# Cross-attention and a mixture-of-experts layer on one core: the hand-over to the experts and the last sum, rearranged

## The reference, cut to what matters

```python
x = x + xattn(layernorm(x), ctx)              # x: (16, 256, 128), ctx: (16, 64, 128), 16 heads of 8
# softmax over the HEADS: attn = softmax(scores, axis=1)
h = layernorm(x)
raw = h @ centroids.T                          # 8 routed experts
scores, balanced = sigmoid(raw), sigmoid(raw + bias)
top_idx = top_k(balanced, 2)
top_w = softmax(gathered scores)               # two gates per token
x = x + h + shared(h) + sum_k top_w[k] * expert[top_idx[k]](h)
# an expert: gelu(h @ Wfc.T) @ Wproj.T, 128 -> 512 -> 128; two shared ones see every token
```

## Time and profile before

| what | value |
|---|---|
| runs | 399.82, 398.01, 400.16 us; median 399.82 |
| the profiled execution | 399.42 us, its span 397.5 us |
| busy PE / PEld | 313.9 us (79%) / 252.4 us |
| busy DVE / ACT / POOL | 288.0 / 259.7 / 260.2 us |
| mean granted TensorE clock | 0.943 |
| chain that ended last | PE 43%, DVE 20%, issue 17%, POOL 7%, ACT 6%, DMA 4% |

### The profile page before, as it was taken

One profiled execution on the slowest core, in us unless ns is written; L12 is line 12 of the kernel. 1 busy time (PEld: TensorE's weight loads), 2 busy tenths in 40 slices (PEclk: granted clock), 3 DMA queues, 4 the chain that ended last, 5 costly groups with the idle time before them and its releaser, 6 DMA issues.

```text
span 397.5 us, 11426 instructions
## 1 busy us (share of the span) xinstructions
PE 313.9 (79%) x3924; PEld 252.4 (63%) x3925; DVE 288.0 (72%) x596; ACT 259.7 (65%) x488; POOL 260.2 (65%) x268
## 2 busy tenths in 40 slices
PE   5865796577676639999999999799999999999100
PEld 1562464354444338888888776698998989999100
DVE  3779999988999967863749555567676667676167
ACT  2788799487686622856344789567666766767075
POOL 6254779789788591577777776057777777777500
PEclk9999899988989985999999999999999999999955
DMA  7956343400000000011112621313333232331097
GB/s 250 333 149 256 106 128 113 121 15 2 2 2 2 2 0 2 26 54 52 55 52 62 153 56 48 97 53 88 86 91 82 70 99 72 82 89 48 7 374 254
DMA packets 29176, 36.12 MB, mean 91 GB/s; under 512 B 4932, under 2 KB 24007, under 8 KB 28624
## 3 DMA queue, kind: packets, MB, share of 16 engines
q1 hardware_dynamic: 24592, 27.13, 22.2%
q0 software_dynamic: 4544, 8.44, 6.7%
HBM read 21.74 MB, written 14.72 MB: 92 GB/s over the span
## 4 chain that ended last, share of the span: by engine, by line
PE 43%; DVE 20%; issue 17%; POOL 7%; ACT 6%; DMA 4%; POOLq 1%; SPq 1%; DVEq 0%; ACTq 0%
PE banks L1454 9%; POOL results L507 7%; DVE Z L907 6%; DVE Mx L902 4%; PE banks L1438 3%; PE banks L1439 3%; PE banks L1440 3%; PE banks L1554 2%; PE banks L1556 2%; PE banks L1540 2%; PE banks L1558 2%; DVE X L1219 2%; ACT E L631 2%; PE banks L1344 2%; PE banks L1542 2%
## 5 line engine op out<-in xcount | busy, mean ns | idle before, releaser
L507 POOL DMA_INDIRECT results<-E,qRep x78 | 86.0, 1102 | 42.3 <-issue 27.4
L489 POOL DMA_INDIRECT gathered<-xs,slot x64 | 64.9, 1014 | 31.0 <-issue 18.6
L1190 DVE TENSOR_TENSOR E<-hid,E 128x512 f16<-128x512 f32 x78 | 54.0, 692 | 36.1 <-ACT E L774 36.1
L435 POOL TENSOR_TENSOR E<-E,rZ 128x1024 f32<-128x1024 f32 x32 | 67.4, 2129 | 18.4 <-DVE rZ L910 18.4
L772 ACT ACTIVATE hid<-banks 128x512 f32<-128x512 f32 x78 | 46.9, 602 | 38.0 <-DVE E L1190 22.6
L1554 PE MATMUL banks<-wprojL,E 128*128 x312 | 54.6, 219 | 2.9 <-DVE E L1190 1.8
L1558 PE MATMUL banks<-wprojH,E 128*128 x312 | 54.2, 219 | 0.0
L1556 PE MATMUL banks<-wprojH,E 128*128 x312 | 54.2, 219 | 0.0
L631 ACT ACTIVATE E<-banks 128x1024 f32<-128x1024 f32 x32 | 33.1, 1095 | 21.8 <-PE banks L1322 21.8
L774 ACT ACTIVATE E<-banks 128x512 f16<-128x512 f32 x78 | 47.2, 605 | 0.0
L1540 PE MATMUL banks<-qRep,wfcH 128*128 128x256 f16 x156 | 42.6, 273 | 0.8 <-ACT E L774 0.5
(11 more groups left out here) (218 smaller groups left out, 823.0 us busy)
## 6 DMA issues: line engine op xcount, KB each, us to landing
qRep<-gathered SPq DMA_DIRECT2D x39, 129.0 KB, 2.2
qRep<-q_rows SPq DMA_DIRECT2D x32, 128.0 KB, 2.5
qRep<-results SPq DMA_DIRECT2D x8, 512.0 KB, 7.3
X<-in_x SPq DMA_DIRECT2D x4, 512.0 KB, 6.6
q_rows<-qRep SPq DMA_DIRECT2D x8, 256.0 KB, 2.1
out<-X SPq DMA_DIRECT2D x8, 256.0 KB, 4.1
results<-E,qRep POOLq DMA_INDIRECT x78
gathered<-spare SPq DMA_DIRECT2D x9, 129.0 KB, 3.9
```

What stands on the lines that cost most here:

```text
L435: g.tensor_tensor(heads, heads, rZ[:, k % 2, :].unsqueeze(1).unsqueeze(3).broadcast_to([P, HH // 2, P, 2]), ALU.mult).then_inc(attn_ready, 1)
L489: g.indirect_dma_start(out=gathered, out_offset=bass.IndirectOffsetOnAxis(ap=slot[:, k, i:i + 1], axis=0), in_=xs[:, i, :], in_offset=None ...
L507: g.indirect_dma_start(out=results, out_offset=bass.IndirectOffsetOnAxis(ap=xg[:, k, h, 2 * D:ROW].bitcast(I32), axis=0), in_=yg[:, k, h, ...
L1190: v.tensor_tensor(gL[:, j, 2 * c:2 * c + 2], hid[:, 2 * j + c].rearrange("p (c q) -> p c q", c=2), gH[:, j, 2 * c:2 * c + 2], ALU.subtract ...
```

## The change

Four edits. (1) ScalarE's copy_o(14) goes ahead of the sigmoids' Exp and of all Gelus; copy_o(15) stays behind the four Gelus. (2) VectorE does scores_in(0) ahead of add_attention(13), and scores_in (for both portions) reads the scores out of PSUM twice, without the copy between. (3) ranks(0) goes from chunk 0 of the first shared expert to chunk 1. (4) For pairs 1 and 4, the last sum is made by TensorE: ScalarE makes 16 diagonal matrices ahead of time (identity times gate: two pairs, two gates, four tiles), TensorE adds X and both diagonal products in a PSUM bank (12 fp32 products a pair), and ScalarE copies the bank into X. VectorE's and ScalarE's own loops do the other six pairs; SP still stores in the order of the pairs.

```diff
+PE_PAIRS = (1, 4)
@@ sync
             for a in range(PAIRS):
-                sp.wait_ge(combined, a + 1)
+                summed = sum(p <= a for p in PE_PAIRS)
+                if a in PE_PAIRS:
+                    sp.wait_ge(copied, summed)
+                else:
+                    sp.wait_ge(combined, a + 1 - summed)
                 sp.dma_start(ov[:, a], Xo[:, a]).then_inc(stored, 16)
@@ scalar
-            sigmoid_exps(0)
-            gelu(0, 0, 0, False)
             act.wait_ge(y_ready, UNITS - 3)
             copy_o(UNITS - 2, 0)
-            for c in range(1, FC):
-                gelu(0, 0, c, False)
+            sigmoid_exps(0)
+            gelus(0, 0, False)
...
             act.wait_ge(gate_ready, 2)
+            for quarter in range(QUARTERS):
+                act.wait_ge(scattered[quarter], 16 * 2 * QT)
+            for n, a in enumerate(PE_PAIRS):
+                for k in range(2):
+                    for i in range(TP):
+                        last = s.activation(diag[:, n, k, i], ident[:], ACT.Identity, bias=zero[:],
+                                            scale=gate[:, k, a * TP + i:a * TP + i + 1])
+                last.then_inc(diag_ready, 1)
+
+            def copy_sum(n):
+                act.wait_ge(sum_ready, n + 1)
+                s.activation(X[:, PE_PAIRS[n]].rearrange("p b c d -> p (b c d)"), sum_ps[n], ACT.Copy).then_inc(copied, 1)
+
             for a in range(PAIRS):
+                if a in PE_PAIRS:
+                    continue
...
                 last.then_inc(gated, 1)
+                for n, b in enumerate(PE_PAIRS):
+                    if a == b + 2:
+                        copy_sum(n)
@@ vector
-            add_attention(UNITS - 3, 1, PAIRS - 2)
...
-                then(v.tensor_copy(rt[:, 0, t], raw))
-                v.tensor_copy(rt[:, 1, t], rt[:, 0, t]).then_inc(rneed, 1)
-                v.tensor_tensor(rt[:, 2, t], rt[:, 0, t], bias8[:].unsqueeze(1).broadcast_to(tok8), ALU.add
+                v.tensor_copy(rt[:, 1, t], raw).then_inc(rneed, 1)
+                v.tensor_tensor(rt[:, 2, t], raw, bias8[:].unsqueeze(1).broadcast_to(tok8), ALU.add
                                 ).then_inc(rneed, 1)
...
             scores_in(0)
+            add_attention(UNITS - 3, 1, PAIRS - 2)
             add_attention(UNITS - 2, 0, PAIRS - 1)
...
-            for a in range(PAIRS):
+            for n, a in enumerate(a for a in range(PAIRS) if a not in PE_PAIRS):
@@ tensor
-            shared_expert(0, 0, 0, 0, False, first=True, ranks_at=(0, 0))
+            shared_expert(0, 0, 0, 0, False, first=True, ranks_at=(0, 1))
...
+            for n, a in enumerate(PE_PAIRS):
+                pe.wait_ge(diag_ready, n + 1)
+                pe.wait_ge(acc_done, PAIRS)
+                pe.wait_ge(yk_loaded[a], 16)
+                for i in range(TP):
+                    o = sum_ps[n][:, P * i:P * i + P]
+                    t.matmul(o, ident[:], X[:, a, i // 2, i % 2, :], start=(i == 0), stop=False, skip_group_check=True)
+                    for k in range(2):
+                        last = t.matmul(o, diag[:, n, k, i], yk[:, a, k, i], start=False, stop=(i == TP - 1 and k == 1),
+                                        skip_group_check=True)
+                last.then_inc(sum_ready, 1)
```

More of the change, by code:

```diff
@@ L190, in xattn_moe_kernel @@
         sharedH, sharedL = (q_flat[:, at:at + 1024].rearrange("p (e n) -> p e n", e=SHARED) for at in (8192, 9216))
+        diag = xs_flat[:, 0:len(PE_PAIRS) * 2 * TP * P * 2].bitcast(F32).rearrange("p (a k i m) -> p a k i m", k=2, i=TP, m=P)
         iota8 = sb("iota8", [P, EXPERTS])
@@ L209, in xattn_moe_kernel @@
                            for i in (0, 1))
+        sum_ps = [banks[:, i, :] for i in range(len(PE_PAIRS))]
         up_ps = [banks[:, i, :] for i in (0, 1, 2, 3)]
@@ L263, in xattn_moe_kernel @@
         combined, combined_half = sem("combined"), sem("combined_half")
+        diag_ready, sum_ready, copied = sem("diag_ready"), sem("sum_ready"), sem("copied")
         stored = sem("stored")
@@ L1221, in _ @@
                 last.then_inc(combined_half, 1)
-                dve.wait_ge(combined_half, a + 1)
-                dve.wait_ge(gated, a + 1)
+                dve.wait_ge(combined_half, n + 1)
+                dve.wait_ge(gated, n + 1)
                 xv = X[:, a].rearrange("p b c d -> p (b c d)")
```

## The result

The changed kernel takes **393.23 us** (median of six runs, 391.42 to 395.13) against 399.48 (six runs, 397.96 to 400.39): a ratio of 0.9845, interval 0.9807 to 0.9883. Forecast were 392.8 in 391.0 to 396.0. The profiled executions took 399.42 and 391.42; the second is the fastest of its six, so the traces differ by more than the medians' 6.2 us. Where a kernel's runs fall into a fast and a slow group, a ratio here compares the fast ones alone and can differ from the quotient of the medians.

The account below looks back on a forecast made before the run. Two lines, TensorE's work and GpSimd's scatters, meet at the routed experts and were taken as the bound, so both must come earlier. 399.42 − 5.1 (earlier start there) − 1.5 (the end) = 392.8 us, range 391.0 to 396.0.

Parts of the forecast that it names:

- 5.1 + 1.5: Gains in us: routed experts start 5.1 earlier (3.5 to 6), and the end is 1.5 shorter.
- VectorE's two steps: scores_in, held by GpSimd at 1.31 and 2.15 us, would take 0.29 and 0.42 reading PSUM.
- ScalarE's order: At the hand-over, copy_o(14) first lets project_out(14) start at 143.5 instead of 149.21; copy_o(15) runs 147.3 to 147.7.
- TensorE's clock: A short clock fall at the hand-over: project_out(15) takes 2.08 us; TensorE's line gains 6.2 us (5 to 7).
- Choose beside GpSimd's small steps: At the hand-over, GpSimd's small steps delay VectorE's choice by 0 to 1.4 us, taken as 0.5.
- Slots: place(0)'s slots ready at 157.1 instead of 161.74, so the scatters' line gains 4.7 us (3.5 to 5.5).
- Which line sets the routed experts' start: The scatters' line sets it: loads land at 247.0, TensorE ready at 246.0, start 247.1 instead of 252.22.
- TensorE's first transpose waiting for it, not for VectorE: Sign at the routed experts' start: TensorE waits for SP's first load, issued at 244.5.
- hangs on these same two lines and moves along: The scatters' later waits, place(1) and the second token rows, were taken to shift with both lines, without separate price.
- The end: Two pairs summed on TensorE: last addition ends at 393.3 against 394.92; 1.5 us gained, bounds 1.6 loss to 2.3 gain.
- rival A's third case: At the end, the full DMA queue sets the time, so no gain there; 394.3 to 395.9 us; whole rival's chance 0.17.
- Rival D: TensorE's sum holds the end and the kernel gets slower, 401.4 us at 9 us a pair; chance 0.03.

Follow-up runs that it names:

- scores_alone: Kernel before plus only scores_in reading PSUM twice and going ahead of add_attention(13); ScalarE's order and ranks as before; profiled run 391.42 us.
- held_scores: Whole change, but scores_in copies out of PSUM once and works on that copy in SBUF, as before; profiled run 394.21 us.
- hand_only: Whole change without the sums on TensorE, the end as in the kernel before; ratio 0.9878 to the kernel before, 394.08 us.
- rows_later: Whole change with VectorE's second_rows(3) moved from behind half expert 11 to behind half expert 12; profiled run 391.24 us.
- plus_one3: rows_later, plus ScalarE instead of VectorE adding the 1 to the sigmoids' Exp, and copy_o(15) ahead of the fourth Gelu; profiled run 390.00 us.
- ranks_first: Whole change, but ranks(0) back in chunk 0 of the first shared expert, as before; profiled run 395.18 us.
- copy_alone: Kernel before plus only ScalarE's copy_o(14) ahead of the sigmoids and Gelus; profiled run 396.09 us.
- no_last_sum: Whole change with the last weighted sum left out, each store waiting for its load alone, output incomplete; profiled run 392.07 us.
- end_only: Kernel before plus only pairs 1 and 4 summed on TensorE, hand-over as before; ratio 0.9959, 396.79 us.

## Why the prediction was right, and where not

The time was forecast as 392.8 and came out at 393.2, by 5.1 + 1.5 where the traces have 5.6 + 1.3. Errors inside both terms partly cancelled, so that the sum came so close is in part luck (below).

- *VectorE's two steps.* Right: priced 0.29 and 0.42, measured 0.29 and 0.28, unheld, and the Exp came at M + 5.5, as by the forecast (copy_o(14) over at 143.5). scores_alone and held_scores show the hold as the cause.
- *ScalarE's order.* Right in each start, to 0.1 us. What the prediction did not work out is how the edits share the gain: it told the story of both holds and priced only their sum. Edit 2 alone gives 5.2, and edit 1 on top of it nearly nothing, since project_out(15) then starts at M + 9.69 with either order, behind GpSimd's last half.
- *TensorE's clock.* Wrong: a short fall was taken into the sum, and the clock stayed at 1.00 through the hand-over, in the change, hand_only, rows_later, plus_one3 and scores_alone. The first down products started 10.7 after M, not 11.8, and TensorE's line was 7.1 us ahead, not 6.2 and just beyond the upper bound of 7. It did fall where TensorE stood 1.9, 2.2 or 3.6 us: held_scores, ranks_first, copy_alone.
- *Choose beside GpSimd's small steps.* Over-priced: 0.5 taken, and from the end of its first step to the end of the choice it took 5.3 us, as before. GpSimd's steps grew instead: five of the fourteen took 0.25 to 0.29, one of them before. The first step's hold was foreseen (its end at M + 8.5, measured 8.56). The Trainium skill (SBUF — State Buffer, Who interferes with whom) fits what was measured of the long instructions, 1.40 for the tensor_scalar in SBUF, which the section counts among the operations that can take a two-port mode, and 2.24 for the sum with two SBUF inputs; of a hold by the small ones VectorE's durations show nothing.
- *Slots.* 4.7 to gain by the forecast, 5.4 measured; the difference is these two terms.
- *Which line sets the routed experts' start.* Wrong in its form: "TensorE's first transpose waiting for it, not for VectorE". TensorE waited for VectorE. The scatters did set the start, but through second_rows(3), a wait in VectorE's queue in front of the low halves that TensorE needs, which the prediction passed over as "hangs on these same two lines and moves along". It does move, with the scatters and not with TensorE, and passed TensorE's surplus back to it. rows_later takes it away, and then the load is what TensorE waits for. Here two errors cancelled: SP's first load came 5.8 us earlier instead of 4.7, and from it to the first transpose 3.25 us passed instead of the forecast's 2.6.
- *The end.* The size was right and its make-up not. The sum ended 2.2 us sooner instead of 1.6, where the loads landed earlier (the last 12.9 us behind the first issue, 14.1 before) and TensorE's sums took 4.6 and 2.7 us, not 5.3 and 3.5. That the loads were earlier for want of stores between them, as the prediction's bound had it, is not shown: in no_last_sum, with seven stores issued before the last load landed, it landed after 13.1, and in rows_later, with the change's stores, after 13.8. But the last store took 3.1, not 2.1, and took back 1.0. That term was wrong in this trace and right in three others with the same end (2.2), whose cause is open; over the six traces with the new end the mean gain is 1.6, and end_only's runs have 1.6 as well (0.41% of 399.36). no_last_sum puts DMA's own need at 19.0, which is rival A's third case, half true: it does not cancel the gain, it caps it.
- *Rival D.* Out. The products of the dearer sum took 4.6/12 = 0.38 us on average and 1.42/3 = 0.47 at the dearest, at clock 0.50 (first tile 374.80, second 376.22); the rows at that clock had 0.42 to 0.52, and 0.66 would have been needed.

## What to carry to other kernels

Beside a busy GpSimd a short VectorE instruction on SBUF can cost the rest of GpSimd's long one: here steps of 0.3 us took 1.31 to 2.24. Look for durations that end just behind another engine's instruction; a source in PSUM, or the step on a third engine, frees them. Before pricing a reordering, ask what a cure of the held step alone would give. And when two lines meet, list every wait by which one of them reaches the other's queue on a third engine, not the last one only: here a copy of 0.17 us behind a wait for scatters took back about 0.9 us. Last, before giving a cause to one trace's tail, read the same number in every trace of the same code: the last store's 3.1 us looked explained until others had 2.2.

## What the runs showed that I had not expected

The clock's price on this path: a wait of TensorE of 2.2 us in ranks_first was followed by 3.4 us at 0.50, so that a stall of 1.5 us cost 3.2; yet 2.4 us of waiting in scores_alone was followed by none. At the end of the change the clock was back 3 to 4 us after TensorE had started its sums at 374.80 (0.50 over 377 to 378, 0.88 over 378 to 379, 1.00 from there on). And in the DMAs, 6.29 MB in and out took 19.0 us from the first issue to the end, against 18 to 18.5 by the rate of the busy microseconds.
